# Layer 0's expert rows: gathered by token number instead of scattered, with the routing cut into pieces between attention steps

## What is computed

```python
xn = _layernorm(x)
s = _L0_attn_ref(xn, ...)          # 16 heads, windows of 64 tokens, relative bias, projection
g = _silu(_L0_ffn_ref(xn, ...))
x = x + s * g
...                                # layer 1: another attention, 8 experts, top 2
```

```python
C = ceil(1.25 * T / E)                               # 160
logits = xt @ w_router
probs = softmax(logits);  top1 = argmax(probs);  gate = probs[top1]
pos = cumsum(onehot(top1), axis=0)[arange(T), top1] - 1
accepted = pos < C
slot = where(accepted, top1 * C + pos, E * C)
buf = zeros((E * C + 1, H)).at[slot].set(xt)         # a table of 5120 rows, 32 x 160
g, u = buf @ w_gate, buf @ w_up
y = (silu(g) * u) @ w_down
out_tok = where(accepted, y[slot] * gate, 0);  return xt + out_tok
```

## Time and profile before

| | us |
|---|---|
| median of 3 runs (lowest, highest) | 1410.75 (1410.49, 1410.78) |
| the profiled execution's own time | 1424.7 |
| its span, first to last instruction | 1422.9 |
| mean granted TensorE clock | 0.900 of full |
| busy: PE, DVE, ACT, POOL | 1195.4, 664.7, 545.7, 322.3 |
| chain that ended last: PE, DVE, ACT | 62%, 12%, 6% of the span |

### The profile page before, as it was taken

How to read it: one execution, slowest core, us unless ns; L and a number is a source line. 1 busy time by engine, 2 the same in 40 slices (tenths; PEclk the granted TensorE clock), 3 DMA queues, 4 the chain that set the end, 5 groups by cost and what they waited for, 6 DMA issues and landing times.

```text
span 1422.9 us, 16582 instructions
## 1 busy us (share of the span) xinstructions
PE 1195.4 (84%) x6125; PEld 1029.2 (72%) x6125; DVE 664.7 (47%) x1490; ACT 545.7 (38%) x1081; POOL 322.3 (23%) x320
## 2 busy tenths in 40 slices
PE   4943789999999997757399999999999999999940
PEld 4822678777777786646387888888888888888940
DVE  7283457666666564875766445445350000000027
ACT  1311333333343332633215565565543232323444
POOL 1026000000000122440251323223232232322200
PEclk8776799999999998855659999999999999999975
DMA  9103123323333224343232334244255496545856
GB/s 324 55 26 107 59 90 95 99 87 112 99 97 96 76 78 143 104 148 118 85 120 92 107 149 169 96 162 158 95 192 215 165 360 264 204 185 199 334 174 210
DMA packets 97553, 204.49 MB, mean 144 GB/s; under 512 B 10014, under 2 KB 82112, under 8 KB 92352
## 3 DMA queue, kind: packets, MB, share of 16 engines
q1 hardware_dynamic: 83632, 166.74, 33.9%
q0 software_dynamic: 13840, 36.68, 7.2%
HBM read 162.77 MB, written 41.68 MB: 144 GB/s over the span
## 4 chain that ended last, share of the span: by engine, by line
PE 62%; DVE 12%; ACT 6%; issue 5%; DMA 4%; SPq 2%; POOL 2%; another core or an unknown queue 1%; POOLq 0%; ACTq 0%; DVEq 0%
PE PS L937 16%; PE PS L927 14%; PE PS L860 5%; PE PS L779 4%; PE PS L819 4%; PE PS L757 3%; PE PS L832 2%; PE PS L767 2%; PE PS L829 2%; PE PS L902 2%; PE PS L888 2%; PE PS L800 2%; PE PS L744 2%; PE PS L735 1%; ACT L1669 1%
## 5 line engine op out<-in xcount | busy, mean ns | idle before, releaser
L927 PE MATMUL PS<-xgT,WE 128*128 128x256 f32 (+1 forms) x1280 | 263.7, 363 | 7.7 <-ACT hT L1669 4.7
L937 PE MATMUL PS<-WE,hT 128*128 128x256 f32 x1152 | 255.2, 379 | 0.0
L927 PEld LDWEIGHTS PS<-xgT,WE 128*128 128x128 f32 x1280 | 225.4, 192 | 41.3 <-ACT hT L1669 10.7
L937 PEld LDWEIGHTS PS<-WE,hT 128*128 128x128 f32 x1152 | 216.8, 190 | 28.4
L1458 DVE TENSOR_TENSOR y<-PS,WE 128x512 f32<-128x512 f32 (+1 forms) x40 | 25.5, 638 | 443.3 <-PE PS L937 443.3
L1669 ACT ACTIVATE hT<-PS,WE 128x256 f32<-128x256 f32 (+1 forms) x320 | 141.4, 452 | 224.4 <-PE PS L927 211.1
L1774 POOL DMA_INDIRECT result<-y,result_of x72 | 71.9, 998 | 303.6 <-DVE y L1458 293.8
L1555 ACT ACTIVATE prob<-sc 128x512 f32<-128x512 f32 x64 | 40.3, 630 | 190.4 <-DVE sc L1134 139.4
L1717 POOL DMA_DIRECT2D result<-y x32 | 18.1, 564 | 335.0 <-DVE y L1183 335.0
L860 PE MATMUL PS<-XT,Wf 128*128 128x256 f32 x384 | 90.2, 393 | 2.2 <-DMA Wf<-wf_dram 1.6
L1763 POOL DMA_INDIRECT xg<-xn_dram,token_of x72 | 80.5, 1117 | 28.8 <-issue 28.8
(11 more groups left out here) (222 smaller groups left out, 1810.6 us busy)
## 6 DMA issues: line engine op xcount, KB each, us to landing
WE<-in_experts SPq DMA_DIRECT2D x40, 2180.0 KB
X<-in_x SPq DMA_DIRECT2D x16, 512.0 KB, 6.2
wgt<-in_w_gate SPq DMA_DIRECT2D x32, 256.0 KB, 3.0
wgt<-in_w_up SPq DMA_DIRECT2D x32, 256.0 KB, 3.4
wgt<-in_w_down SPq DMA_DIRECT2D x32, 256.0 KB, 2.8
both<-result SPq DMA_DIRECT2D x16, 512.0 KB, 8.7
table<-zeros POOLq DMA_DIRECT2D x1, 5120.0 KB, 20.9
rows<-table SPq DMA_DIRECT2D x40, 128.0 KB
```

What stands on the lines that cost most here:

```text
L927: m = e.matmul(PS[:, FIRST_H_BANK + nth % HR, 0:rows], W1[n % WR][:, k, c * P:(c + 1) * P], xgT[:, n % 2, k, 0:rows], start=k == 0, stop=k ...
L937: m = e.matmul(PS[:, u.bank, j * D:(j + 1) * D], hT[:, n % 2, c, j * P:(j + 1) * P], W2[n % WR][:, c, :], start=c == 0, stop=c == KF - 1)
```

## The change

1. The table in DRAM, its zeros, the scatter and SP's 40 loads go. XN of each group is stored to `xn0_dram` by SP. The routing ends in `token0_of`, the token number of each row of the 40 tiles, found as in layer 1; GpSimd gathers each tile by it, through four buffers, four ahead of its use. A row without a token reads token 0's.
2. The routing is eight items, one a step, in steps 0 to 7; experts start at step 7 as before.
3. Layer 0's normalizing is ScalarE's: x * rstd + shift, with `shift0` from VectorE.
4. The start is listed anew: "fold" right behind the first group's norm; q, k and v in the first round; scores 0 and 1 inside the third and fourth round. SP loads what "fold" needs behind the second quarter of x.

```diff
-            if g:
-                normalized(0, g - 8)
-                add("logits0", g - 8)
-                yield
-        normalized(0, g)
-        add("logits0", g)
-        add("route0_best")
...
+    def routing():
+        for what in ("best", "hot", "count", "put", "rows", "rows_known", "get", "gate"):
+            add(f"route0_{what}")
+            yield

     def experts():
         add("load0_first")
+        for n in range(RR):
+            add("load_rows0", n)
...
-    advance(first, 3)
-    add("q_bias")
-    add("q", 0)
-    add("k", 0)
-    add("v", 0)
+    add("stats", 0, 0)
+    add("norm", 0, 0)
     add("fold")
-    advance(first, 3)
-    add("score", 0)
-    add("score", 1)
+    for g in range(0, NT, 8):
+        if g + 8 < NT:
+            add("stats", 0, g + 8)
+        add("turn", 0, g)
+        add("logits0", g)
+        if g == 0:
+            add("q_bias")
+            for what in "qkv":
+                add(what, 0)
+        if g + 8 < NT:
+            add("norm", 0, g + 8)
+        if g >= 16:
+            add("score", g // 8 - 2)
     for s in range(STEPS + 5):
...
-        advance(first)
+        advance(route)
```

TensorE's and VectorE's part of the new items ("route0_rows_known" then subtracts 1, takes the larger of that and 0 and converts to integers, three passes over 40 columns; `RR` is 4, `TILES0` 40, `ROWS_AT_ONCE` 8):

```diff
+            elif what == "route0_rows":
+                u = use["route0_rows",]
+                fill_from(u)
+                for i in range(NT // ROWS_AT_ONCE):
+                    w.wait_ge(hot_tile0_ready, i + 1)
+                    w.wait_ge(hot_row0_ready, i + 1)
+                    for j in range(ROWS_AT_ONCE):
+                        m = e.matmul(PS[:, u.bank, 0:TILES0], hot_row0[:, i % 2, j, :], hot_tile0[:, i % 2, j, :],
...
+                    if (i + 1) * ROWS_AT_ONCE < NT:
+                        m.then_inc(hot0_used, 1)
...
+            if layer == 0:
+                e.scalar_tensor_tensor(out=shift0[:, g:g + 8], in0=mean_var[:, g:g + 8, 0], scalar=-1.0,
+                                       in1=rstd[:, g:g + 8], op0=ALU.mult, op1=ALU.mult).then_inc(ln_shift, 1)
+                return
...
-                e.tensor_copy(slot_put[:, :], pos0[:, :]).then_inc(put_ready, 1)
+                e.tensor_copy(slot0_i[:, :], pos0[:, :]).then_inc(put_ready, 1)
+                w.wait_ge(put_ready, 1)
+                e.tensor_scalar(tile0_i[:, :], slot0_i[:, :], P.bit_length() - 1, None, ALU.logical_shift_right).then_inc(
...
+                e.tensor_copy(tile0_f[:, :], tile0_i[:, :]).then_inc(route, step.step())
...
+                e.scalar_tensor_tensor(out=in_tile0[:, :], in0=tile0_f[:, :], scalar=-float(P), in1=pos0[:, :],
+                                       op0=ALU.mult, op1=ALU.add).then_inc(rows0_cut, 1)
+            elif what == "route0_rows":
+                w.wait_ge(rows0_cut, 1)
+                for i in range(NT // ROWS_AT_ONCE):
...
+                    if i >= 2:
+                        w.wait_ge(hot0_used, i - 1)
+                    e.tensor_tensor(hot_tile0[:, i % 2, :, :],
...
+                    e.tensor_tensor(hot_row0[:, i % 2, :, :],
```

ScalarE, GpSimd and SP:

```diff
+            elif what == "norm" and at[0] == 0:
+                g = at[1]
+                w.wait_ge(ln_shift, g // 8 + 1)
+                for t in range(g, g + 8):
+                    e.activation(XN[:, t, :], X[:, t, :], ACT.Identity, bias=shift0[:, t:t + 1],
+                                 scale=rstd[:, t:t + 1]).then_inc(ln_xn, 1)
...
+        def load_rows0(n):
+            w.wait_ge(rows0_known, 1)
+            w.wait_ge(xn0_saved, 16 * (NT // 8))
+            w.wait_ge(ln_xn, NT)
+            if n >= RR:
+                u = use["rows", n - RR]
+                w.wait_ge(full[u.bank], u.filled)
+            e.indirect_dma_start(
+                out=rows0[:, n % RR, :], out_offset=None, in_=xn0_dram,
+                in_offset=bass.IndirectOffsetOnAxis(ap=token0_of[:, n:n + 1], axis=0), bounds_check=T - 1,
+                oob_is_err=False).then_inc(rows_in[n % RR], 16)
...
-                for t in range(NT):
-                    e.indirect_dma_start(
-                        out=table0, out_offset=bass.IndirectOffsetOnAxis(ap=slot_put[:, t:t + 1], axis=0),
-                        in_=XN[:, t, :], in_offset=None, bounds_check=SLOTS0 - 1, oob_is_err=False).then_inc(scattered0, 16)
...
+            elif what == "rows":
+                n, = at
+                if n + RR < TILES0:
+                    load_rows0(n + RR)
...
+            if q == 1:
+                e.dma_start(dft[:, :, :], a["dft"].rearrange("(k p) n -> p k n", p=P)).then_inc(dft_in, 16)
...
-                w.wait_ge(scattered0, 16 * NT)
                 w.wait_ge(ln_xn, NT)
-                load_rows0(0)
-                load_rows0(1)
...
+            elif what == "norm" and at[0] == 0:
+                g = at[1]
+                w.wait_ge(ln_xn, g + 8)
+                e.dma_start(xn0_view[:, g:g + 8, :], XN[:, g:g + 8, :]).then_inc(xn0_saved, 16)
```

More of the change, by code:

```diff
@@ L123 @@
 FIRST_TILES = 8
+RR, TILES0, ROWS_AT_ONCE = 4, SLOTS0 // P, 8
 FIRST_EXPERT_STEP = 7
@@ L160, in add @@
                 banks.take(("total0", i), 6 + i)
+        elif what == "route0_rows":
+            banks.take(item, 4)
         elif what == "fold":
@@ L167, in add @@
             banks.take(item, 4)
-    def normalized(layer, g):
-        add("norm", layer, g)
-        add("turn", layer, g)
-    def start():
-        for g in range(0, NT, 8):
-            add("stats", 0, g)
-            if g:
-                normalized(0, g - 8)
-                add("logits0", g - 8)
-                yield
-        normalized(0, g)
-        add("logits0", g)
-        add("route0_best")
-        yield
-        add("route0_count")
-        yield
-        add("route0_put")
-        yield
-        add("route0_get")
-        yield
-        add("route0_gate")
-        yield
+    def routing():
+        for what in ("best", "hot", "count", "put", "rows", "rows_known", "get", "gate"):
+            add(f"route0_{what}")
+            yield
     def experts():
         add("load0_first")
+        for n in range(RR):
+            add("load_rows0", n)
         for n in range(GT):
@@ L248, in advance @@
         return [next(generator, generator) for _ in range(n)][-1] is generator
-    first, ffn, combine = start(), experts(), combination()
-    advance(first, 3)
-    add("q_bias")
-    add("q", 0)
-    add("k", 0)
-    add("v", 0)
-    add("fold")
-    advance(first, 3)
-    add("score", 0)
-    add("score", 1)
+    route, ffn, combine = routing(), experts(), combination()
+    add("stats", 0, 0)
+    add("norm", 0, 0)
+    add("fold")
+    for g in range(0, NT, 8):
[11 more added lines that the diff above has]
+            add("score", g // 8 - 2)
     for s in range(STEPS + 5):
@@ L422, in build @@
     rstd = place("rstd", [P, NT])
+    shift0 = place("shift0", [P, NT])
     NB = D + 1
@@ L439, in build @@
     work = top[0]
-    top[0] = SBUF_END - 12 * D
-    zeros = place("zeros", [P, D])
-    top[0] = work
     router0 = place("router0", [P, KD, E0])
@@ L463, in build @@
     reset0 = place("reset0", [P, E0, NT])
+    assert top[0] <= work
+    top[0] -= 3 * 4 * E0 * NT
+    hot_row0 = place("hot_row0", [P, 2, ROWS_AT_ONCE, P])
+    hot_tile0 = place("hot_tile0", [P, 2, ROWS_AT_ONCE, TILES0])
     assert top[0] <= work
@@ L483, in build @@
     top[0] = persistent_top
-    rows0 = place("rows0", [P, 2, D])
+    rows0 = place("rows0", [P, RR, D])
     rowsT = place("rowsT", [P, 2, KD, GROUP * CAP])
@@ L488, in build @@
     hT0 = place("hT0", [P, 2, KD, CAP])
+    best0 = place("best0", [P, NT])
+    slot0_i = place("slot0_i", [P, NT], I32)
+    tile0_i = place("tile0_i", [P, NT], I32)
+    tile0_f = place("tile0_f", [P, NT])
+    in_tile0 = place("in_tile0", [P, NT])
+    row0_v = place("row0_v", [P, TILES0])
     assert top[0] <= xn_base
@@ L725, in tensor @@
                                  stop=True).then_inc(full[u.bank], 1)
+            elif what == "route0_rows":
[6 more added lines that the diff above has]
+                        m = e.matmul(PS[:, u.bank, 0:TILES0], hot_row0[:, i % 2, j, :], hot_tile0[:, i % 2, j, :],
+                                     start=i + j == 0, stop=(i + 1) * ROWS_AT_ONCE + j + 1 == NT + ROWS_AT_ONCE)
+                    if (i + 1) * ROWS_AT_ONCE < NT:
+                        m.then_inc(hot0_used, 1)
+                m.then_inc(full[u.bank], 1)
             elif what in ("q", "k"):
@@ L1781, in sync @@
         w = Waits(e)
-        def load_rows0(n):
-            if n >= 2:
-                u = use["rows", n - 2]
-                w.wait_ge(full[u.bank], u.filled)
-            e.dma_start(rows0[:, n % 2, :], table0[n * P:(n + 1) * P, :]).then_inc(rows_in[n % 2], 16)
         def load_gate_up(ex):
@@ L1831, in sync @@
                     load_down(ex)
-            elif what == "rows":
-                n, = at
-                if n + 2 < SLOTS0 // P:
-                    load_rows0(n + 2)
             elif what == "load_down":
```

91 lines of the change are left out of this document (58 added, 33 removed).

## The result

The kernel after took 1425.09 us (median of 4 runs, 1422.57 to 1426.40) and the kernel before 1410.76 (4 runs, 1410.49 to 1412.04) beside it: a ratio of 1.0098, 95% interval 1.0080 to 1.0115. It is slower by 14 us, where 1401.2 and a range of 1388 to 1416 were forecast. One fact has to stand ahead of all that follows: the kernel before, with nothing in it changed, took about 1410 us in some sets of executions and about 1426 in others, on the same chip too. The profile ahead of the prediction (1424.7) looks like the second kind; the median that it was set beside is of the first.

What follows compares the result with a forecast made beforehand. TensorE bounds the long stages; the change touches only what lies before about 170 of 1422.9 us. Step 8's score at 149.5 + 10.0 = 159.5 against 169.0, 9.5 off the median 1410.75, gives 1401.2 us; range 1388 to 1416.

Steps and rivals of the forecast that it cites:

- The profiled execution took 1424.7 [...]; the runs' median is 1410.75, 14 less. I take the difference over as it is: Whole kernel: the 9.5 us gain summed on the profile was taken off the runs' median, giving 1401.2 us.
- Scatter, zero fill and their wait go: Layer 0, 118.6 to 138.0 us: the nearly idle stretch leaves with the scatters; 18 us gained, bounds 0 and 18.
- code loading beside the burst: Inferred cause of the 19.4 us idle stretch: engines run out of instructions while the 32 scatters run.
- The rule that I set against it: DMA engines alternate between queues packet by packet, so code packets don't wait behind a burst and the stall may stay.
- the stall stays: Rival: the idle stretch only changes place, hanging on instruction count; price 18 to 20 us, 1420 us; chance 0.10.
- The start is ordered anew: Start of layer 0, until score 1 is in PSUM: ends at 80.0 us, between 73.6 and 86.3.
- Routing in pieces: Score 1 to step 7's score: VectorE queue 58.5, row-product wait 8, rest 3 us; ends at 149.5 against 157.9.
- Row loads move from SP to GpSimd: Score of step 7 to step 8: the 3.0 us row-load wait goes, 1.9 comes back; 10.0 us against 11.1.
- Later gathers: The 36 gathers after the first row tiles, in GpSimd's queue: cost nothing; uncovered 1.3 us each, 47 at most.
- TensorE held behind the pieces: Rival: half clock in late logits and row products; start 86.3, row products 12.1 more; 6 us slower, 1417; chance 0.12.
- The rival with the clock on its side: Start and row products at full clock: start 73.6, wait 3.4, 20.5 us gained, 1390 us; chance 0.14.

Runs made afterwards that it cites:

- e9: Kernel before, unchanged, run again for a profile of an execution near 1410 us: 1409.7 us, profiled 1410.5.
- e2: Kernel before without its 32 scatters and the wait for them; experts read rows of zeros: 1400.0 us, 0.981 of the kernel before.
- e16: Repeat in another set of the kernel before with its scatters sent to a tensor nobody reads or waits for: 1426.6 us beside a kernel before of 1426.5.
- e8: Kernel before with its 32 scatters sent to a tensor nobody waits for, experts reading zeros: 1397.1 us, in a set where the kernel before took 1410.
- e3: Gather alone: rows gathered by token number, whole routing ahead of the first score, start of before, VectorE normalizing: 1421.65 us, kernel before at 1426.
- e4: Kernel after with the start's order of before and VectorE normalizing; gather and routing in pieces kept: 1413.1 us, kernel before at 1426.
- e14: Repeat in another set of gather alone, with whole routing ahead and the start of before: 1423.6 us, kernel before at 1426.
- e15: Repeat in another set of gather and pieces with the old start order and VectorE normalizing: 1414.5 us, kernel before at 1426.
- e18: Repeat of gather, pieces, old start, VectorE normalizing and bfloat16 row products: 1405.5 us, 0.986 of a kernel before of 1426.5.
- e13: Kernel before with the first two experts' weights loaded ahead of the wait for the scatters' end: 1428.3 us beside 1426.3.
- e17: Repeat in another set of the kernel before with weights loaded ahead of the wait for the scatters' end: 1427.9 us beside 1426.5.
- e10: Kernel after with VectorE normalizing layer 0 again, the new order of the start kept: 1423.3 us.
- e6: Kernel after with only the start's order of before; ScalarE still normalizes: 1422.7 us.
- e7: Gather and pieces with the old start and VectorE normalizing, row products in bfloat16 (one pass in place of two): 1405.9 us, 0.9976 of the kernel before.

## Why the prediction was wrong

**The step that failed** is "The profiled execution took 1424.7 [...]; the runs' median is 1410.75, 14 less. I take the difference over as it is", together with the 18 us for "Scatter, zero fill and their wait go". The 14 us were the stretch itself. An execution of 1410.5 has none (e9), and there the scatter costs 8 us of open wait in front of the eleventh score: without the stretch the seventh score comes 21 us earlier, and 14 are left after that wait. I took the gain from the execution that had the stretch and the end time from runs that had not. Against the right trace the sum reads: eleventh score at 159.5 against 155.0, 4.5 us slower, 1415. The same working, set beside an execution of the kind that was timed, forecasts a slower kernel. What is left of the miss is 9.4 us of sizes: 6.1 in the start, 0.5 in the pieces, 1.2 in the row loads and 1.6 behind the eleventh score. The warning was in my own two numbers: a profile 14 us above three runs that agree within 0.3 us.

**What the stretch is.** My inference, code loading beside the burst, is neither shown nor excluded. It needs the scatters (e2 has none of it in a set where the kernel before had it); it does not need anybody to wait for them (e16); instruction packets come late in it, but they may follow from the stall as well as cause it, and no run parts the two. Why it is absent in whole sets of executions, on the same chip, is open. The rule that I set against it, from the Trainium skill, DMA: Bandwidth & Descriptors, section Queues, rings and completion order, gave no stall hanging on the burst. If the stall is one of code loading, the executions with it speak against that use of the rule: there the second packet came 11 to 16 us after the first, with the scatter at 29% of the DMA engines in e16. e8 and e9, with the same burst, speak for it. The rival built on it, that the stall stays, did not happen: e3, e4, e14, e15 and e18 have gathers only, ran beside a kernel before of 1426, and no such stretch is in their profiles.

**"The start is ordered anew"**: 80.0 forecast, 86.06 measured, inside its ends of 73.6 and 86.3. Fold and ScalarE's normalizing were 4.4 us too short (26.1 against 30.5), and two errors partly cancel in that: the fold began at 10.3 and not 14.9, beside the normalizing, and took 20.2 us where it was priced at 11.2, its duration at full clock late in the old start; as TensorE's first work it ran at half clock. One short group of logits came as forecast. The execution of 73.07 lands near the lower end by luck: that end had all logits short, and there two of four took 6.9 and 6.3, while the fold took 13.1.

**"Routing in pieces"**: 69.5 us forecast from the second score to the tenth, 70.0 measured, and that is luck. The wait that the row products add, taken as 8 between 3.4 and 12.1, was 12.3 (2.27, 1.79 and 8.23), the end of the half clock; VectorE was busy 2.0 us less than forecast, and its other gaps and waits were 3.1 where 4.9 were allowed. And the gain I booked was against 61.1 us that held the stretch; the kernel before without it takes 39.5. Pieces do help, by 8.5 to 9 us against the same routing in one piece (e3 and e4, e14 and e15). What they repay is the price of the row numbers, which the scatter never needed: e3 has its first score at 116.1 where e9 has it at 94.4, both with three long groups of logits (2.7 of these 21.7 us are the later first turn).

**"Row loads move from SP to GpSimd"**: 10.0 forecast, 11.2 measured, no wait for a gather as forecast; against 19.0 of an execution without the stretch, this is the change's gain, 7.8. The 1.1 us that the step was to give beside the profile's 11.1 did not come. **Later gathers**, costed at nothing: from the eleventh score to the end it is 1255.3 us against 1253.7 in e9, so 1.6. That stretch takes 1253.7 to 1254.8 in the profiles of the kernel before and of e13, e16 and e17, and 1254.2 to 1257.8 in those with gathers, so a price of the gathers is not settled by this.

The account against e9, in the times of the eleventh score: second score 10.4 ahead (the routing stood in front of it before), second to tenth score 30.5 behind, step 8 7.8 ahead, the rest 1.6 behind: 13.9, which is the difference of the spans, 1422.6 and 1408.7. In whole kernels beside 1410: gather alone about +12, pieces -9, order of the start +9.5 (e10 against e4 and e15), ScalarE's normalizing +1.6 on top of that order; with the old order it alone is +9.6 (e6). The first two were measured beside a kernel before of 1426; that they hold beside 1410 rests on e7, the one version without scatter that was timed in both kinds of set.

The rival of the other side, TensorE held behind the pieces, had the start (86.3) and the row products (12.1) right and gave 1417; it failed by the same step. The rival with the clock on its side had its case too, the execution of 1409.37, and that was still no faster than before. The kernel after itself was not timed in a set where the kernel before takes 1426. There I would expect no difference; that is argued, not shown.

## What to carry to other kernels

Before a sum is made against a profile, set its time beside the runs; if it is a per cent off, the profile has something the runs don't, and the largest stall without a semaphore is the first suspect. Price a removed stall only from an execution that is as long as the timed ones. In every profile here without matmuls put ahead, TensorE's first work ran at half clock, turns or fold; a stage that is moved to the front should be priced so. And a version whose time does not hang on such a stall (here gather, pieces, the old start and bfloat16 row products) is worth more than its median says.

## What I had not expected of the hardware

The same program took 1397.1 us in one set of executions and 1426.6 in another (e8 and e16); within the first its four times lie within 4 us. The window up to 50.8 us of the kernel after gives a clock of 1.00, while its fold products took 3.77 us where they take 1.99: in these first 50 us durations tell the clock and that column doesn't. And 8.5 us of matmuls ahead of the fold left 8 of 12 executions at 1420 us or above.
